# Four-bit weights quantised inside rope attention, and a one-column root as ScalarE's last operation in six stages

## The reference, cut to what matters

```
x = x + 0.5 * ffn(_layernorm(x))
x = x + attn(_layernorm(x))
x = x + 0.5 * ffn(_layernorm(x))
```

```
def fp4_quant_dequant(x):            # blocks of 16 along the last dimension
    scale = maximum(max(abs(xb)) / 6.0, 1e-12)
    xn = xb / scale
    q = _GRID[searchsorted(_MID, abs(xn))] * sign(xn) * scale    # grid 0, .5, 1, 1.5, 2, 3, 4, 6
def fp4_linear(x, w): return einsum('bsk,nk->bsn', fp4_quant_dequant(x), fp4_quant_dequant(w))
h = silu(fp4_linear(x, w_gate)) * fp4_linear(x, w_up)
return fp4_linear(h, w_down)         # 128 -> 352 -> 128
```

## Time and profile before

| | us |
|---|---|
| median of 3 runs | 2228.85 |
| lowest, highest | 2224.99, 2229.91 |
| the profiled execution | 2229.42 |
| its span in the profile | 2227.6 |
| granted TensorE clock, mean | 0.926 |
| busy: PE, DVE, ACT, POOL | 1850.9, 1673.5, 1167.8, 1038.5 |

### The profile page before, as it was taken

The page is one execution under the profiler, slowest core; times in us unless marked ns, Lnnn a source line. Parts: engine busy times, 40 slices in busy tenths (PEclk is TensorE's granted clock), DMA queues, the critical chain, the costliest instruction groups (busy, mean ns, idle before and its releaser), DMA issues. The chain is left out here.

```text
span 2227.6 us, 35911 instructions
## 1 busy us (share of the span) xinstructions
PE 1850.9 (83%) x11912; PEld 1457.0 (65%) x11943; DVE 1673.5 (75%) x4293; ACT 1167.8 (52%) x2191; POOL 1038.5 (47%) x904
## 2 busy tenths in 40 slices
PE   4888877968888789968997997987993579999856
PEld 3666663746666667746776885676882467777734
DVE  7899974879989787766777775667777856777786
ACT  3777753237777565535555553344553246666332
POOL 4898851238999555543554662003662321111022
PEclk9999999979999989987997998998996879999977
DMA  3000000000000034306432441003430010000000
GB/s 124 1 1 1 1 12 2 3 1 1 1 1 1 1 92 119 114 5 151 121 115 60 130 128 40 1 0 90 132 116 0 1 49 1 1 2 1 1 1 20
DMA packets 57187, 91.48 MB, mean 41 GB/s; under 512 B 8664, under 2 KB 19736, under 8 KB 56880
## 3 DMA queue, kind: packets, MB, share of 16 engines
q1 hardware_dynamic: 57008, 89.25, 14.2%
HBM read 87.34 MB, written 1.88 MB: 40 GB/s over the span
## 5 line engine op out<-in xcount | busy, mean ns | idle before, releaser
L1041 POOL TENSOR_TENSOR unit_hid_low<-unit_hid,unit_hid_high 128x512 fp32r<-128x512 f32 x272 | 352.7, 1297 | 274.9 <-ACT unit_hid_high L1217 274.9
L800 DVE SCALAR_TENSOR_TENSOR pk_chosen<-bank,pk_least,pk_sums 128x1024 f32<-128x1024 f32 x256 | 325.0, 1271 | 46.0 <-issue 37.2
L665 ACT COPY pk_sums<-bank 128x1024 f32<-128x1024 f32 x256 | 261.2, 1021 | 124.7 <-PE bank L563 124.4
L563 PE MATMUL bank<-pk_pick,pk_sim_both 128*128 128x512 f32 x512 | 191.0, 455 | 104.4 <-DVE pk_chosen L800 104.3
L479 POOL TENSOR_TENSOR pk_chosen<-pk_chosen 128x1024 f32<-128x1024 f32 (+1 forms) x126 | 265.7, 2112 | 13.5 <-DVE pk_chosen L800 13.5
L1098 PE MATMUL bank<-unit_x_high,units_high 128*128 128x512 f32 x544 | 222.4, 409 | 19.1 <-ACT unit_gact L1210 7.9
L1099 PE MATMUL bank<-unit_x_low,units_high 128*128 128x512 f32 x544 | 217.4, 400 | 0.0
L1100 PE MATMUL bank<-unit_x_high,units_low 128*128 128x512 f32 x544 | 217.1, 399 | 0.0
L1217 ACT CAST unit_hid_high<-unit_hid 128x512 fp32r<-128x512 f32 x272 | 166.8, 613 | 57.3 <-DVE unit_hid L1367 28.9
L563 PEld LDWEIGHTS bank<-pk_pick,pk_sim_both 128*128 128x128 f32 x512 | 78.8, 192 | 162.0 <-DVE pk_chosen L800 125.8
L578 PE MATMUL bank<-ident,pk_chosen 128*128 128x128 f32 x1152 | 150.0, 277 | 0.0
(11 more groups left out here) (405 smaller groups left out, 4463.1 us busy)
## 6 DMA issues: line engine op xcount, KB each, us to landing
unit_comb<-comb_dram SPq DMA_DIRECT2D x136, 256.0 KB, 3.2
unit_comb<-comb_dram SPq DMA_DIRECT2D x272, 128.0 KB, 3.1
raw<-in_geglu_units SPq DMA_DIRECT2D x3, 774.0 KB, 6.7
raw<-in_swiglu_units SPq DMA_DIRECT2D x3, 768.0 KB, 8.2
dh_w<-in_de_w SPq DMA_DIRECT2D x1, 1024.0 KB, 6.1
out_x<-x_res SPq DMA_DIRECT2D x1, 1024.0 KB, 5.1
raw<-in_geglu_units SPq DMA_DIRECT2D x1, 967.5 KB, 10.3
raw<-in_swiglu_units SPq DMA_DIRECT2D x1, 960.0 KB, 11.8
```

Source lines behind the costliest of these rows:

```text
L563: ins = nc.tensor.matmul(sums_ps[:, 2 * b + e, :], both[:, i % 2, h, :], pk.pick[:, e * PK_K // 2:(e + 1) * PK_K // 2, :].rearrange("p i j ...
L665: nc.scalar.copy(sums_sb[:, b, :].rearrange("p (e n) -> p e n", e=2), sums_ps[:, 2 * b:2 * b + 2, :]).then_inc(sums_out.sem, 1)
L800: nc.vector.scalar_tensor_tensor(chosen[:, h, :].rearrange("p (e n) -> p e n", e=2), sums_ps[:, 2 * b:2 * b + 2, :], least2[:, i % 2, h:h ...
L1041: nc.gpsimd.tensor_tensor(hid_low[:, i % HB, :], hid[:, i % HB, :], hid_high[:, i % HB, :].bitcast(FP32), ALU.subtract).then_inc(hidden.se ...
```

## The change

Three things change.

1. Each of six stages (product-key, experts, favor, rope, four-bit ffn, decay) ends on ScalarE with `load_square_root`: a root of one column of ones into a tile that nobody reads. Position attention doesn't get one. Stages that are called several times do it each time.
2. The quantising stage is gone; its work is spread over the engines' lists in the second Block of rope attention. GpSimd clears the padding first. VectorE finds the scales of both parts ahead of its wait for rope's tables. GpSimd does the rounding behind its batch loop, with other operations than before: the step comes from comparisons of the squared value with 4 and 16 instead of bit masks. TensorE turns the nine chunks behind its batch loop, and ScalarE copies them behind its own, ahead of its root.
3. The weight loads are issued in the first SwiGLU stage instead of the second.

```diff
+    def load_square_root(self, act):
+        self.nc.scalar.activation(self.unused[:], self.ones[:, 0:1], ACT.Sqrt)
...
             read_product(NT - 1)
+            k.load_square_root(act)
...
-def rope_attention(k, a):
+def rope_attention(k, a, f4):
...
         def _(pool):
+            f4.clear(pool)
+            nc.gpsimd.drain()
             nc.gpsimd.memset(zeros[:], 0.0)
...
                 nc.gpsimd.tensor_copy(xb[:], k.xnT[:, bass.ts(b, T)]).then_inc(x_in.sem, 1)
+            f4.round(pool)
...
                     if 1 <= u <= U:
                         turn(u - 1)
+            f4.turn(pe)
...
                         read_high(u - 1)
+            f4.read_turned(act)
+            k.load_square_root(act)
...
         def _(dve):
 
+            f4.find_scales(dve)
             dve.wait_ge(loaded.sem, loaded.at(80))
...
+    def find_scales(self, dve):
+        dve.wait_ge(loaded.sem, loaded.at(16 * 7))
+        dve.wait_ge(cleared.sem, cleared.at(1))
+        for f, w in self.parts:
+            nc.vector.tensor_reduce(f.scale[:], blocked(w), axis=AX.X, op=ALU.max, apply_absolute_value=True)
+        nc.vector.drain()
+        for f, w in self.parts:
+            nc.vector.tensor_scalar(f.scale[:], f.scale[:], 1.0 / F4_MAX, F4_SCALE_MIN, ALU.mult, ALU.max)
+        nc.vector.drain()
+        for f, w in self.parts:
+            nc.vector.reciprocal(f.inv[:], f.scale[:])
+        nc.vector.drain()
+        for f, w in self.parts:
+            nc.vector.tensor_scalar_mul(f.inv[:], f.inv[:], F4_TIES_DOWN).then_inc(scaled.sem, 1)
+
+    def round(self, pool):
+        pool.wait_ge(scaled.sem, scaled.at(2))
+        for f, w in self.parts:
+            near, step = f.near[:], f.step[:].bitcast(FP32)
+            nc.gpsimd.tensor_tensor(blocked(near), blocked(w), over(f.inv[:]), ALU.mult)
+            nc.gpsimd.drain()
+            nc.gpsimd.tensor_tensor(w, near, near, ALU.mult)
+            nc.gpsimd.drain()
+            nc.gpsimd.tensor_scalar(step, w, 4.0, F4_ROUND, ALU.is_ge, ALU.mult)
+            nc.gpsimd.tensor_scalar(w, w, 16.0, 2.0 * F4_ROUND, ALU.is_ge, ALU.mult)
+            nc.gpsimd.drain()
+            nc.gpsimd.tensor_tensor(step, step, w, ALU.add)
+            nc.gpsimd.drain()
+            nc.gpsimd.tensor_scalar(step, step, F4_ROUND, None, ALU.add)
+            nc.gpsimd.drain()
+            nc.gpsimd.tensor_tensor(near, near, step, ALU.add)
+            nc.gpsimd.drain()
+            nc.gpsimd.tensor_tensor(near, near, step, ALU.subtract)
+            nc.gpsimd.drain()
+            nc.gpsimd.tensor_tensor(blocked(w), blocked(near), over(f.scale[:]), ALU.mult).then_inc(rounded.sem, 1)
...
+                experts_ffn(k, ew, f4.load)
+                rope_attention(k, a, f4)
                 experts_ffn(k, ew)
-                rope_attention(k, a)
-                experts_ffn(k, ew, f4.load)
-        f4.quantise()
         fp4_ffn(k, f4)
```

More of the change, by code:

```diff
@@ L68 @@
     comb_in_0 comb_in_1 comb_in_2 comb_in_3 comb_in_4
-    loaded set_up f4_loaded f4_rounded f4_turned dh_loaded
+    loaded set_up f4_loaded f4_cleared f4_scaled f4_rounded f4_turned dh_loaded
     x_in
@@ L2369, in _ @@
                         add((u - 3) // H)
+    f4.passed()
     loaded.passed(80)
@@ new lines, in scratch, with clear @@
+    def scratch(self, ctx):
+        self.f_rows, self.f_cols = Fp4Scratch(self.k, ctx, 6 * P), Fp4Scratch(self.k, ctx, F4_I)
+        self.parts = ((self.f_rows, self.rows[:].rearrange("p i c d -> p (i c d)")), (self.f_cols, self.cols[:]))
+    def clear(self, pool):
+        self.k.nc.gpsimd.memset(self.rows[F4_CHUNKS[2][1]:P, :, 2, :], 0.0).then_inc(self.k.counter("f4_cleared").sem, 1)
+    def find_scales(self, dve):
+        nc, loaded, cleared, scaled = self.k.nc, self.loaded, self.k.counter("f4_cleared"), self.k.counter("f4_scaled")
+        dve.wait_ge(loaded.sem, loaded.at(16 * 7))
[11 more added lines that the diff above has]
+            nc.vector.tensor_scalar_mul(f.inv[:], f.inv[:], F4_TIES_DOWN).then_inc(scaled.sem, 1)
@@ new lines, in turn @@
+    def turn(self, pe):
+        k, nc, rounded, turned = self.k, self.k.nc, self.k.counter("f4_rounded"), self.k.counter("f4_turned")
+        pe.wait_ge(rounded.sem, rounded.at(2))
+        for i in range(2):
+            for c, (at, n) in enumerate(F4_CHUNKS):
+                nc.tensor.transpose(k.bank[i][:, at:at + n], self.rows[0:n, i, c, :], k.ident[0:n, 0:n])
+        for c, (at, n) in enumerate(F4_CHUNKS):
+            ins = nc.tensor.transpose(k.bank[2][0:n, c * P:(c + 1) * P], self.cols[:, at:at + n], k.ident[:])
+        ins.then_inc(turned.sem, 1)
@@ new lines, in read_turned, with passed @@
+    def read_turned(self, act):
+        k, nc, turned = self.k, self.k.nc, self.k.counter("f4_turned")
+        act.wait_ge(turned.sem, turned.at(1))
+        for i in range(2):
+            nc.scalar.copy(self.up[:, i, :], k.bank[i][:, 0:F4_I])
+        for c, (at, n) in enumerate(F4_CHUNKS):
+            nc.scalar.copy(self.down[0:n, c, :], k.bank[2][0:n, c * P:(c + 1) * P])
+    def passed(self):
+        self.loaded.passed(16 * 7)
+        for name, n in (("f4_cleared", 1), ("f4_scaled", 2), ("f4_rounded", 2), ("f4_turned", 1)):
+            self.k.counter(name).passed(n)
```

40 lines of the change are left out of this document (5 added, 35 removed).

## The result

| | before | after |
|---|---|---|
| median, us (runs) | 2226.92 (4) | 2214.40 (4) |
| lowest, highest | 2224.77, 2229.91 | 2212.01, 2216.96 |
| ratio, 95% interval | | 0.9942, 0.9930 to 0.9954 |
| the profiled execution, its span | 2229.42, 2227.6 | 2216.96, 2214.9 |
| granted TensorE clock, mean | 0.926 | 0.930 |

Faster by 12.5 us, by the interval 10.2 to 15.6; 2215.5 was forecast. A later job with the same kernel gave 2213.83 (6 runs) beside 2226.95 (17 runs). The page's first part hardly moves against the earlier trace rows: GpSimd has 26.7 us more work, VectorE 3.9 less.

The account below looks back on a forecast made before the run. It took serial stretches between barrier-closed stages as what the change touches (TensorE 83%, VectorE 75% busy). -16.0 - 3.1 - 0.6 + 0.6 + 4.4 + 1.3 = -13.4 us from the median 2228.85 gave 2215.4; it forecast 2215.5, range 2210.5 to 2221.5.

Parts of the forecast that it names:

- The quantising stage: Between the second SwiGLU and first four-bit stages: its serial stretch goes, next VectorE start 1695.03 to 1679.01, -16.0 us.
- Rope's end: Behind rope attention's last product: transposes 2.1, copies 1.3, load and root 1.48, nothing covering them; +4.4 us.
- rival D: At the stage tails: the table load costs the drain as well, +4.1 us, time 2219.5; chance 0.04.
- Contention: In rope attention: GpSimd's rounding holds up the first rotation (+0.9) and late two-input operations (+0.4); +1.3 us.
- rival E: In rope attention: GpSimd's constant operations far slower than a copy, and L2330 held up; slower, 2240 at 56 us; chance 0.05.
- Rival B: In rope attention: GpSimd's rounding holds up the one-column negated maximum L2330 too; time 2220, chance 0.2.
- Rope's start: Start of rope attention: padding and scales hidden in VectorE's 7.46 idle, DMA wait swallows the root's 1.04; 0 us.
- a sign against it: In rope attention: a first projection earlier than 9 us after the stage's start would show a term wrong.
- The product-key ends: Ends of the two product-key stages: with the load ScalarE would end 0.3 later than VectorE, twice; +0.6 us.
- The loads: Seven weight loads moved from the last SwiGLU stage to the first: cost 0, about 1 us if exposed.
- The starts: Roots no longer wait for table loads: position and both four-bit starts 1.04 each (-3.1), two experts starts 0.28 each (-0.6).

Follow-up runs that it names:

- b3: The changed kernel with the one-column root only at the end of the experts and decay stages; 2212.05 us, ratio 0.9938.
- e2: The changed kernel without any of its six roots, so only the quantising work is moved; 2220.29 us, ratio 0.9954.
- e3: The changed kernel with the negated row maximum computed over two columns instead of one; 2213.08 us, ratio 0.9931.
- b2: The kernel before with the one-column root only at the end of the experts and decay stages; 2221.02 us, ratio 0.9968.
- e1: The kernel before with all six one-column roots, quantising stage kept; 2222.25 us, ratio 0.9970.
- e4: The changed kernel with transposes and copies moved to the next experts stage's start and no root at rope's end; 2212.94 us, ratio 0.9934.
- a1: The changed kernel unaltered, run again; 2213.83 us beside 2226.95 for the kernel before, ratio 0.9945.
- c2: The changed kernel with two more passes of GpSimd's rounding operations, results unused; 2218.45 us, ratio 0.9963.
- c4: The changed kernel with thirty more two-input GpSimd operations behind the rounding; 2216.72 us, ratio 0.9945.
- c3: The changed kernel with twenty more GpSimd operations with a constant behind the rounding, results unused; 2218.38 us, ratio 0.9960.

## Why the prediction was right, and where it was not

**The quantising stage, -16.0.** Held. SwiGLU 2 takes 187.6 in three executions and 171.5 in nine of eleven with the move: -16.1.

**Rope's end, +4.4.** The step was right, its size too high. The tail grew by 3.30. Of that the load and root are 1.50 (3.62 against 2.12 in b3 and e2), as forecast. Copies took 1.3. The transposes took 1.1, from 1509.72 to 1510.82, instead of the 2.1 they took in the quantising stage, where TensorE had stood idle for 14.82 us; here it came from work. The granted clock was 0.50 there (1.2 GHz) and 1.00 here (2.4 GHz), as windows over the transposes show, before and after:

```profile
1691.30:1693.50 2.20, 2.08 (x9) 1.65 (x9) 0.00 (x0) 0.06 (x1) 0.00 (x0) 0.50 0.00 0
...
1509.72:1510.85 1.13, 1.10 (x11) 0.85 (x9) 0.29 (x1) 0.00 (x0) 0.00 (x0) 1.00 0.00 0
```

A duration at the lower clock was carried to a place with the full one.

**No drain.** The 1.50 for load and root also answers rival D: by the 2.66 us of the Trainium skill (ScalarE: Activation LUTs, What ACT_TABLE_LOAD costs) this part would be 1.4 longer. The trace agrees with the page's 1283 ns for the load itself, but shows no drain: the load begins as the last copy ends, at 1512.16, and the root follows it by 0.02.

**Contention, +1.3.** Held in kind, a little small by the pair with its repetition: body +2.0 (141.5 against 139.5). Over all six bodies with this code it is +1.6 (141.15 on average). The rotation lost 0.92 (forecast 0.9), two maxima 0.87 (forecast 0.4), because the rounding took 29.1 us instead of 20 to 24. What was wrong is the operation with a constant: 2.79 us for 768 columns, where I took a copy's 0.9 with an upper bound of 1.8. The bound was wrong too. It cost little, for the slow operations hold VectorE off for only 0.7 us each; rival E, which had them at 3.3 us and more, needed L2330 held up as well, and it wasn't.

**The negated maximum.** Rival B falls: 154 ns throughout, and e3 shows that two columns would be held up. The 14 ns of the earlier trace rows were a sign of it. The Trainium skill (VectorE: DVE Perf Modes, Mode 2×_2P) asks for outermost dimensions, those of length one left out, that are even or match. The prediction left those words out; the page doesn't say what holds for a single column, which has no such dimension. In the trace one column was never held up.

**Rope's start, 0.** Held, in part by chance: the root is 1.05 earlier and the first rotation is where it was (12.55 before, 12.49 after). The projections began 8.58 after the stage's start, not 9.03, which the prediction had named as a sign against it. The tables' landing released them in both, and that doesn't follow the root: the projections began 8.74 after the start with it (b2) and 8.73 without (e2, where GpSimd's mask came last), and 7.76 to 9.04 over all kernels. The 0.45 was lost again, since from there to the first rotation TensorE took 3.92 at a granted clock of 0.50, against 3.52 at 0.60 before. The scales are hidden: VectorE still idles 3.03 behind them.

**The product-key ends, +0.6.** 0.26 each, 0.5. **The loads, 0.** Held, as far as this shows: the first SwiGLU stage, which has them now, takes 173.45, 172.24 and 173.04 in the three executions without them, and in the eleven with them 172.25 to 173.40, at the same two levels. No run was made for it.

**The starts, -3.7.** At the seams they are as forecast: a root with its set loaded runs 0.03 behind the variance, instead of 1.08 at four starts and 0.31 at two. The times of whole kernels are not. Roots alone gave 6.2 and 7.1 us, and both intervals exclude 3.4; adding them to the move gave about 6 by the medians (2220.29 to 2213.83 and 2214.40, from different jobs), but by the ratios (0.9954 to 0.9945 and 0.9942) only 2.0 to 2.7. By the table the three starts that gain average 43.9, 89.2 and 93.8 in twelve executions with the roots against 45.8, 90.3 and 95.5 in two without: 1.9, 1.2 and 1.7, where I had 1.04 each. TensorE's clock has a part in it, but its mean over a stage doesn't set the stage's length. Windows of the position stage in e1, e2, b3 and e4 (us; then busy time per engine; clock, DMA share, GB/s):

```profile
955.42:997.07 41.65, 29.81 (x144) 20.12 (x144) 30.74 (x107) 12.47 (x33) 18.74 (x17) 0.88 0.03 8
```

```profile
959.35:1006.71 47.36, 32.67 (x144) 23.33 (x144) 33.13 (x107) 13.81 (x34) 18.69 (x17) 0.82 0.03 7
```

```profile
959.14:1002.00 42.86, 31.10 (x144) 21.69 (x144) 31.60 (x108) 12.47 (x33) 18.74 (x17) 0.82 0.03 7
```

```profile
956.16:1000.60 44.44, 29.96 (x144) 21.00 (x144) 32.80 (x107) 12.57 (x33) 18.70 (x17) 0.88 0.03 7
```

The same 144 products take 29.8 and 30.0 at 0.88, 31.1 and 32.7 at 0.82, but the stage is shorter in b3 at 0.82 than in e4 at 0.88. Untouched stages scatter by as much: the first product-key stage is 1.96 shorter in b2 than before. The runs with roots alone had a mean clock of 0.928 against 0.926 of the kernel before, and within the runs of one kernel, over all kernels, 0.001 of clock goes with about 1.0 us, so some 2 us of the difference go with the clock. That the earlier roots cause it was not shown; with two profiles without them, this part stays open.

**Why the sum came out.** Measured at the seams the steps are -16.1 - 3.2 - 0.6 + 0.5 + 3.3 + 2.0 = -14.1, against the forecast -13.4 and the measured -12.5 and -13.1 (a1), whose intervals hold both sums. The steps at the seams were mostly right; that the tail's 1.1 too much and the contention's 0.7 too little nearly cancel is luck. The 3 us that the roots seem to give beyond their seams don't show in the whole: with them the sum would be some -17, outside the first job's 10.2 to 15.6. The move alone gave 8.2 by the medians, with an interval of 6.5 to 14.0, where its steps measure 16.1 - 1.8 (tail without a root) - 1.5 (body) = 12.8. In the one pair of profiles the unchanged stages add their own scatter, as these windows of the first product-key stage, in the changed kernel and in its repetition, show.

```profile
9.33:329.94 320.61, 251.56 (x1552) 205.16 (x1552) 277.98 (x989) 212.93 (x318) 248.25 (x223) 0.97 0.05 16
```

```profile
9.08:325.39 316.31, 247.28 (x1552) 200.79 (x1552) 277.89 (x990) 213.03 (x318) 248.40 (x224) 0.98 0.05 17
```

## What to carry to other kernels

A stage that keeps one engine busy at a time is worth its whole length if its work finds idle time, but what is left of it must not stand behind a stage's last product: the same transposes and copies cost 1.8 us there and nothing at the next stage's start, beside VectorE's measuring. A table load belongs at the end of a stage only where another engine ends later and the next start would wait for it; of six places two gave nearly all. When terms are smaller than the scatter of an untouched stage (4.7 us here), judge them by the seam they act on, since medians of six runs don't rank them, and look there at the granted clock too, since a duration taken at one level doesn't hold at the other.

## What the runs showed of the hardware that was not expected

- A GpSimd operation with a constant is slower than one with two tensors: 2.79 us (two operations, 768 columns) and 2.15 (one) against 1.82.
- It holds VectorE off only until 0.67 to 0.69 us after it began (five cases), while one with two inputs does until 0.13 to 0.15 before its end (c2: at 1379.46, 1399.33, 1447.38).
- The holding off goes both ways. GpSimd's operation with two inputs took 2.07 to 2.08 instead of 1.81 where a rotation had begun before it (c4, five in a row from 1446.91), one with a constant 3.30 instead of 2.78 (c3 at 1452.52), and GpSimd got through 0.13 to 0.15 before the rotation's end.
- A VectorE operation with a constant on one column was never held up (154 ns, up to 156), on two columns up to 1076 ns. In nine executions 102 of them began beside GpSimd's rounding or the added operations.
- One kernel's runs differ within one job by up to 12 us (2221.56 to 2233.80 before, beside a1), and the mean granted clock goes along in part (0.929 in the run of 2222.77, 0.923 in that of 2233.71, beside b2).
